# The complex feed-forward part of a transformer layer: three real products per tile instead of four

## What is computed

```python
xn = _layernorm(x)                                   # x: (32, 2048, 1024)
x = x + attn(xn) + ffn(xn)

# attn: 16 heads, causal, T = 2048
q1, q2, k1, k2 = (xn @ W.T for W in (W1_q, W2_q, W1_k, W2_k))     # 4 numbers per head each
L_q, L_k = exterior(q1, q2), exterior(k1, k2)        # 6 normalised numbers per head
attn = softmax(L_q @ (L_k @ J6.T).T * 6**-0.5, causal)
out = (attn @ (xn @ W_v.T + b_v)) @ W_out.T + b_out  # D = 1024

# ffn: a complex linear map, W_real and W_imag are 512 x 512, each unfolded from two small tensors
W_real, W_imag = unfold(G1_R, G2_R), unfold(G1_I, G2_I)
xr, xi = split(xn, 2, axis=-1)
out_real = xr @ W_real.T - xi @ W_imag.T + bias_real
out_imag = xr @ W_imag.T + xi @ W_real.T + bias_imag
ffn = concatenate([out_real, out_imag])
```

## Time and profile before

| | |
|---|---|
| runs of the kernel | 1768.63, 1771.18 (median) and 1957.53 us |
| the profiled execution, its own time | 1771.96 us |
| its span, first to last instruction, slowest core (core 1) | 1770.9 us |
| spans of the eight cores | 1757.7 to 1770.9 us |
| TensorE busy | 1582.8 us, 89% of the span |
| ScalarE busy | 1210.7 us, 68% |
| VectorE busy | 718.1 us, 41% |
| GpSimd busy | 172.5 us, 10% |

### The profile page before, as it was taken

How to read it: one execution, slowest core, us unless ns; L and a number is a source line. 1 busy time by engine, 2 the same in 40 slices (tenths; PEclk the granted TensorE clock), 3 DMA queues, 4 the chain that set the end, 5 groups by cost and what they waited for, 6 DMA issues and landing times.

```text
span 1770.9 us, 57248 instructions; the slowest of 8 cores (1757.7 to 1770.9 us)
## 1 busy us (share of the span) xinstructions
PE 1582.8 (89%) x24704; PEld 621.0 (35%) x24704; DVE 718.1 (41%) x1343; ACT 1210.7 (68%) x1408; POOL 172.5 (10%) x142
## 2 busy tenths in 40 slices
PE   3657999999988999999988999999997899999998
PEld 2323433333334443333334443333333443333332
DVE  5577534233245543333235553332226554321112
ACT  2434767878853668788774567878883466778786
POOL 1001110100011111000011110110001111012000
PEclk9978989999999999999999999999999999999999
DMA  9421522313235251321223442341223533122101
GB/s 203 97 74 38 117 65 64 88 55 68 73 79 133 73 145 38 97 61 37 75 83 103 122 109 71 75 103 37 56 61 91 145 79 79 38 62 85 38 25 49
DMA packets 159064, 141.20 MB, mean 80 GB/s; under 512 B 128224, under 2 KB 132448, under 8 KB 158816
## 3 DMA queue, kind: packets, MB, share of 16 engines
q1 hardware_dynamic: 154432, 132.75, 29.2%
q0 software_dynamic: 4384, 4.78, 1.8%
HBM read 78.32 MB, written 33.55 MB: 63 GB/s over the span
## 4 chain that ended last, share of the span: by engine, by line
PE 69%; DVE 11%; ACT 11%; issue 6%; DMA 2%; SPq 0%; DVEq 0%; ACTq 0%; POOL 0%; POOLq 0%
PE F L281 34%; PE S L596 14%; PE OA L635 8%; ACT ex L607 8%; PE DN L635 5%; PE OB L635 5%; DVE oT L656 3%; DVE xb L483 2%; DMA wqk<-wqkT 1%; DVE vt L430 1%; ACT rden L648 1%; ACT rden L646 1%; DVE qks L304 1%; DVE vt L519 1%; PE F L559 1%
## 5 line engine op out<-in xcount | busy, mean ns | idle before, releaser
L607 ACT ACTIVATE ex<-S 128x1024 bf16<-128x1024 f32 (+4 forms) x1055 | 1082.3, 1049 | 457.9 <-PE S L596 443.8
L596 PE MATMUL S<-fq,fk 6*128 6x512 bf16 (+3 forms) x2560 | 378.3, 357 | 42.7 <-ACT ex L607 40.4
L451 POOL TENSOR_TENSOR xb<-xb,outb 128x512 f32<-128x512 f32 x122 | 157.3, 1310 | 1506.9 <-DMA xb<-x 1506.9
L281 PE MATMUL F<-wv,xnT 128*32 128x512 bf16 x4096 | 265.1, 388 | 25.2 <-ACT vt L423 12.3
L281 PE MATMUL F<-wo,oT 128*32 128x512 bf16 x4024 | 268.0, 386 | 6.5 <-DVE oT L656 6.5
L635 PE MATMUL OA<-ex,vt 128*32 128x512 bf16 (+3 forms) x2560 | 238.9, 363 | 33.6 <-DVE ex L617 18.1
L596 PEld LDWEIGHTS S<-fq,fk 6*128 6x128 bf16 x2560 | 101.0, 91 | 453.3 <-issue 449.2
L635 PE MATMUL DN<-ex,ones 128*32 128x512 bf16 (+3 forms) x2560 | 235.1, 356 | 0.0
L483 DVE TENSOR_TENSOR xb<-F,xb 128x512 f32<-128x512 f32 x122 | 84.4, 691 | 370.3 <-PE F L281 356.1
L635 PE MATMUL OB<-ex,vt 128*32 128x512 bf16 (+3 forms) x2560 | 234.1, 355 | 0.0
L617 DVE TENSOR_TENSOR ex<-ex,tri 128x512 bf16<-128x512 bf16 x256 | 104.3, 419 | 232.2 <-ACT ex L607 231.7
(11 more groups left out here) (77 smaller groups left out, 844.2 us busy)
## 6 DMA issues: line engine op xcount, KB each, us to landing
xst<-x SPq DMA_DIRECT2D x62, 512.0 KB, 4.6
xb<-x SPq DMA_DIRECT2D x61, 512.0 KB, 4.3
y<-xb SPq DMA_DIRECT2D x60, 512.0 KB, 3.0
wv<-wvT POOLq DMA_DIRECT2D x4, 512.0 KB, 30.2
wo<-woP POOLq DMA_DIRECT2D x4, 512.0 KB, 39.4
ex<-x SPq DMA_DIRECT2D x3, 512.0 KB, 11.0
y<-xst SPq DMA_DIRECT2D x6, 256.0 KB, 2.2
oT<-x SPq DMA_DIRECT2D x2, 512.0 KB, 16.5
```

Source lines behind the costliest of these rows:

```text
L281: ins = TE.matmul(bank[32 * j:32 * j + 32, lo:hi], stationary[:, 32 * j:32 * j + 32], moving, start=start, stop=stop, tile_position=(0, 32 ...
L451: gS.inc(GE.tensor_tensor(r[:, h * 512:(h + 1) * 512], r[:, h * 512:(h + 1) * 512], outb[:, h * 512:(h + 1) * 512], OP.add))
L596: ins = TE.matmul(S[:, m * 512 + off:(m + 1) * 512], fk[32 * m:32 * m + 6, o:o + 128], fq[c % 2][32 * m:32 * m + 6, g * 512 + off:(g + 1) ...
L607: n = sS.inc(SE.activation(view(ex[i % 3], m0 * 512 + off, dims), view(S, m0 * 512 + off, dims), AF.Exp, scale=SCALE))
```

## The change

The complex product is made from three real ones. With `s = -(W_real + W_imag)` and `d = W_imag - W_real`, the common product `C = (xr + xi) @ W_real.T` goes to both halves: `out_real = C + xi @ s.T`, `out_imag = C + xr @ d.T`.

- `wi` and `wn` go, `ws` and `wd` come, and two small buffers `xs` for `xr + xi`.
- `xs_make` adds the two halves of a tile's `xnT` on VectorE (128 x 512, bf16).
- A new unit `common_unit`, one per tile, of 4 pieces, makes `C` in `F`; VectorE then adds the bank to both halves of the residual in one operation of 1024 columns, makes the next tile's `xs`, and only then `background` runs. The wait for the residual moves here from `out_add`.
- `out_products` has four feed-forward pieces instead of eight, so an `out_unit` has 12 instead of 16, an `early_unit` 8 or 10 instead of 12 or 14.
- `ffn_pieces` makes both parts of a block of the weights in five pieces and then `wr`, `ws`, `wd`.
- `choose` weighs the queues by pieces instead of units, takes a short unit (4 pieces or fewer) at the head of `outs` whenever it is asked, and no longer gives up where the head is not ready.

```diff
         def out_products(t, half, bank, groups, ffn):
...
             if ffn:
-                for kc in range(8):
-                    w = (wr, wi)[half] if kc < 4 else (wn, wr)[half]
-                    ins = by_columns(0, 512, xnT_of(t, kc), w[:, (kc % 4) * 512:(kc % 4) * 512 + 512],
-                                     kc == 0, False, bank)
+                for k in range(4):
+                    ins = by_columns(0, 512, xnT_of(t, k + 4 * (half == 0)),
+                                     (ws, wd)[half][:, k * 512:k * 512 + 512], k == 0, False, bank)
                     yield 1.0
...
+        def xs_make(t):
+            o = (t % CH) * 1024
+            x = xnT[(t // CH) % 4]
+            wait_for(VE, xt_in[t])
+            tS.wait(VE, xs_used.get(t - 2, 0))
+            xs_in[t] = vS.inc(VE.tensor_tensor(xs[t % 2][:], x[:, o:o + 512], x[:, o + 512:o + 1024], OP.add))
+
+        def common_unit(t):
+            vS.wait(TE, ffn_in[0])
+            vS.wait(TE, xs_in[t])
+            wait_for(TE, f_free[0])
+            for k in range(4):
+                ins = by_columns(0, 512, xs[t % 2][:, k * 128:k * 128 + 128], wr[:, k * 512:k * 512 + 512],
+                                 k == 0, k == 3)
+                if k == 3:
+                    xs_used[t] = tS.inc(ins)
+                yield 1.0
+            tS.wait(VE, tS.n)
+            gS.wait(VE, xb_in[t])
+            r = view(residual(t), 0, [[512, 2], [1, 512]])
+            n = vS.inc(VE.tensor_tensor(r, view(F, 0, [[0, 2], [1, 512]]), r, OP.add))
+            if t + 1 < NT:
+                xs_make(t + 1)
+            evicted((vS, n))
...
         def out_add(t, half, bank):
             tS.wait(VE, tS.n)
-            gS.wait(VE, xb_in[t])
...
+            def total(ri):
+                for half in (1024, 512):
+                    vS.wait(VE, vS.n)
+                    to = TERM + 1024 if half == 1024 else TERM + 512 * ri
+                    vS.inc(VE.tensor_tensor(fview(to, [[1, half]]), fview(TERM + 1024, [[1, half]]),
+                                            fview(TERM + 1024 + half, [[1, half]]), OP.add))
+                return True
...
+                vS.inc(VE.tensor_copy(w[0], re))
+                vS.inc(VE.scalar_tensor_tensor(w[1], re, -1.0, im, OP.mult, OP.subtract))
+                ffn_in[0] = vS.inc(VE.tensor_tensor(w[2], im, re, OP.subtract))
...
+            return [lambda: products(0), lambda: total(0), lambda: products(1), lambda: total(1), weights]
...
-                self.gen, self.left, self.ready = gen, cost, ready
+                self.gen, self.left, self.ready, self.short = gen, cost, ready, cost <= 4
...
-                    self.outs.extend(Unit(out_unit(prev * CH + t, h), 16.0)
-                                     for t in range(CH) for h in range(2))
+                    for t in range(prev * CH, prev * CH + CH):
+                        self.outs.append(Unit(common_unit(t), 4.0, lambda: not ffn))
+                        self.outs.extend(Unit(out_unit(t, h), 12.0, lambda: not ffn) for h in range(2))
...
-                        self.outs.extend(Unit(early_unit(t, h), 8.0 + 2 * n, lambda n=n: (c, n - 1) in o_in)
+                        self.outs.append(Unit(common_unit(t), 4.0))
+                        self.outs.extend(Unit(early_unit(t, h), 4.0 + 2 * n, lambda n=n: (c, n - 1) in o_in)
...
-                spare = len(self.outs) - self.ends
-                if self.outs and not self.outs[0].ready():
-                    return None
-                if self.outs and (end or not self.vs or 16 * spare > 8 * len(self.vs)):
+                ready = self.outs and self.outs[0].ready()
+                spare = sum(u.left for u in self.outs) - 14 * self.ends
+                if ready and (end or not self.vs or self.outs[0].short
+                              or spare > sum(u.left for u in self.vs)):
                     return self.outs.popleft()
-                for q in (self.vs, self.qk, self.outs):
+                for q in (self.vs, self.qk, self.outs if ready else None):
...
+            if c == 1:
+                xs_make(0)
```

More of the change, by code:

```diff
@@ L85, in build @@
         wr = sb("wr", 4 * 512, BF16)
-        wi = sb("wi", 4 * 512, BF16)
-        wn = sb("wn", 4 * 512, BF16)
+        ws = sb("ws", 4 * 512, BF16)
+        wd = sb("wd", 4 * 512, BF16)
+        xs = [sb(f"xs{i}", 512, BF16) for i in range(2)]
         xnT = [sb(f"xnT{i}", CH * 1024, BF16) for i in range(4)]
@@ L477, in out_products @@
                     yield 1.0
+        xs_in, xs_used = {}, {}
+        def xs_make(t):
[21 more added lines that the diff above has]
+            evicted((vS, n))
         def out_add(t, half, bank):
             tS.wait(VE, tS.n)
-            gS.wait(VE, xb_in[t])
             r = residual(t)[:, half * 512:half * 512 + 512]
@@ L509, in early_unit, with ffn_pieces, done, products @@
             evicted((vS, n))
-        def ffn_pieces(ri, j):
-            w = (wr, wi)[ri][:, j * 512:(j + 1) * 512]
-            def products():
+        def ffn_pieces(j):
+            def done():
+                return fview(TERM, [[1, 512]]), fview(TERM + 512, [[1, 512]])
+            def products(ri):
                 d_g2.wait(VE, d_g2.n)
-                vS.inc(VE.tensor_tensor(fview(TERM, [[512, 4], [16, 32], [1, 16]]),
+                vS.wait(VE, vS.n)
+                vS.inc(VE.tensor_tensor(fview(TERM + 1024, [[512, 4], [16, 32], [1, 16]]),
                                         fview(G1O + (ri * 4 + j) * 128, [[32, 4], [1, 32], [0, 16]]),
@@ L522, in products, with weights @@
                 return True
-            def pairs():
+            def total(ri):
+                for half in (1024, 512):
+                    vS.wait(VE, vS.n)
+                    to = TERM + 1024 if half == 1024 else TERM + 512 * ri
+                    vS.inc(VE.tensor_tensor(fview(to, [[1, half]]), fview(TERM + 1024, [[1, half]]),
+                                            fview(TERM + 1024 + half, [[1, half]]), OP.add))
+                return True
+            def weights():
+                re, im = done()
+                w = [t[:, j * 512:(j + 1) * 512] for t in (wr, ws, wd)]
                 vS.wait(VE, vS.n)
-                vS.inc(VE.tensor_tensor(fview(TERM + 2048, [[1, 1024]]), fview(TERM, [[1, 1024]]),
-                                        fview(TERM + 1024, [[1, 1024]]), OP.add))
-                return True
[L530 to L540, removed]
+                vS.inc(VE.tensor_copy(w[0], re))
+                vS.inc(VE.scalar_tensor_tensor(w[1], re, -1.0, im, OP.mult, OP.subtract))
+                ffn_in[0] = vS.inc(VE.tensor_tensor(w[2], im, re, OP.subtract))
+                return True
+            return [lambda: products(0), lambda: total(0), lambda: products(1), lambda: total(1), weights]
         def bias_unit():
@@ L727, in build @@
         lns.extend(ln_pipeline(range(CH, 2 * CH), True))
-        for ri in range(2):
-            for j in range(4):
-                ffn.extend(ffn_pieces(ri, j))
+        for j in range(4):
+            ffn.extend(ffn_pieces(j))
         background()
```

## The result

The changed kernel takes 1977 us against 1769: the ratio is 1.1177, with a 95% interval of 1.1131 to 1.1224. The forecast was 1910, the range 1840 to 1968. The direction and the place were right, the size was 67 us short and outside the range. Some executions of most of the kernels, the unchanged one too, are several per cent longer, with a lower granted clock on the cores of one die or of both; every ratio here compares executions without that, and e9 (two such executions) and e12 (one) therefore have times and no ratio.

A forecast was written before the change was run, and what follows sets the result against it. TensorE was taken to set the pace, with ScalarE near at w = 3. The terms: 1772 - 49 + 87 + 6 + 13 + 16 + 5 + 4 = 1854, plus 56 for the clock, 1910 us; range 1840 to 1968.

The forecast's parts named there:

- C before O in 31 group ends: Common unit ahead of the output unit at 31 group ends, TensorE idle 3.35 us; +87 outside w = 0, +13 there.
- The seven ends with C behind O8: At w = 2 and 3, common unit behind eight output-unit pieces at seven group ends: 2.6 us idle each, +16.
- all ends: All changed group ends, waits and clock falls together: 106 + 16 + 56 = 178 us.
- Pieces removed ... -49: Four pieces fewer per tile, 55.0 us of TensorE; a third of the 17 us at w = 3 lost: -49.
- eight ends with 4 pieces less: At w = 1, group ends that had 16 pieces now have 12 within the same wait: +6.
- the clock's 56: Clock falls behind the longer idle times at group ends: 33 falls at 1.7 us each, +56.
- 38 falls of 6.8: Upper end of the clock term: 38 falls of 6.8 us at 0.44 per us, 114 us.
- chunk 0's +4: The weights' unfolding in ffn_pieces: more VectorE work in chunk 0, between 0 and 7 us, taken as +4.
- -49 + 5 + 4 = -40: Pieces removed -49, further waits at w = 0 over three chunks +5, ffn_pieces in chunk 0 +4.

The follow-up runs named there:

- e9: Changed kernel without common units: each output unit makes the common product in its own bank, 16 pieces, old order; 1771.0 and 1773.4 us.
- e12: Kernel before with 12 pieces per output unit, half of the feed-forward products left out, nothing added; 1850 us in the profiled execution.
- e3: Kernel before with one wait added: at 31 group ends TensorE waits for normalize before going on with filler work; ratio 1.0814, 1912 us.
- e5: Changed kernel, but at group ends the output unit is taken and the common unit comes at a later step; ratio 1.0261, 1822 us.
- e2: Changed kernel with 14 idle matmuls between common and output unit at each of the 31 ends; ratio 1.0709, 1895 us.
- e7: Kernel before with 14 pieces per output unit, a quarter of the feed-forward products left out, nothing added; ratio 0.9993.
- e1: Changed kernel with a common unit that is first at a group's end issued, with its addition, ahead of normalize; ratio 1.0618, 1877 us.
- e8: Changed kernel with its order at the ends, but 16-piece output units and no common units at w = 3; ratio 1.0792, 1914 us.
- e4: Kernel before with ffn_pieces in the changed kernel's form; ratio 1.0007.
- e6: As e5, but output units at w = 3 make the common product in their own bank, 16 pieces, without common units; ratio 1.0221, 1812 us.
- e10: As e7, but output units at w = 3 and in the last chunk keep all 16 pieces; ratio 0.9891, 1748 us.

## Why the prediction was right and wrong

**Right: the order and what it does.** C before O in 31 group ends, its addition behind `normalize` (802.50 behind 801.90), idle for 3.31 against 3.35, the addition 1.21 long against 1.23. The seven ends with C behind O8 were taken too dear: TensorE waits 1.7 (w = 2) and 1.3 (w = 3) there, not 2.6, and no fall follows on any core. e3 puts the price of these gaps, clock included, at 144 us against 153; e5 puts all ends at 162 against 178.

**Right: the clock follows the gaps, at the price forecast.** e2 gives 0.33 per us at w = 1 (5.5 for 16.5), where the forecast took 0.38. At w = 3 the five of e2's 24 chunks that never fell take 149.9, against 165.9 with 41 us low in the changed kernel, whose delays are the same: 0.39; the line through all 24 of e2 has 0.41.

**Wrong: "Pieces removed ... -49".** This step failed. The term turned 256 x 0.215 us of TensorE into 49 us of the kernel, and asked only where ScalarE is near, not what the removal does to the clock. e7 measured -1 (between -10 and +7). Where the clock never fell, the pieces gave 2.8, 1.7, 2.4 and 2.5 of 3.4 us per chunk, and at w = 3 more than at w = 1; summed over the chunks that is 30 to 35 us, an estimate from the two tables. But the time at the lower level rose from 72 to 127 us per core, which at some 0.4 took 22 of it back, the largest part in the last chunk (7 us longer, 35 us low). And the cores spread: the slowest took 1767, the other seven 1743 to 1748. With twice as many pieces gone the sign turns (e12). So the pieces had been holding the clock up. I treated filler work as a load only. The sum has one more slip: eight ends with 4 pieces less are 6.9 us, not 6.

**Wrong by size: the clock's 56.** I counted 33 falls of 5.1 us, 168 us. Measured are 253 us more than before (325 less 72, mean of the cores). Each of the 31 gaps has a fall on each core, 6.1 long in the mean. 110 of the 253 lie in the three chunks at w = 3, which also have falls of over 15 us: 27 of them on the eight cores, 22 of which begin at key tile 4, three steps behind a group's end. In groups 0 and 2 of chunk 7 no kernel here has filler in the two steps between (key tiles 2 and 3), the kernel before neither; at key tile 4 the kernel before has 4 pieces, the changed one 1. These falls are in the changed kernel, e1, e2, e5 and e12 and hardly in the others. e8 prices w = 3 as a whole at 58 us. The forecast of 152 for such a chunk missed it by 14 (165.9), w = 1 (95 against 99.2) and w = 2 (122 against 125.9) by 4. The range ended at 38 falls of 6.8 and had no case in which a fall lasts 17 us, though the earlier trace rows has one of 13.7.

**Too high: chunk 0's +4.** e4: net about nothing (chunk 0 longer by 11, chunk 1 shorter by 8).

Put together from the measurements: the ends 162 (forecast 178), and 46 in what e5 has left, where the forecast had -49 + 5 + 4 = -40. By the mean of the cores what e5 has left is 51: w = 3 has 3 x 8.7 = 26, w = 0 3 x 2.9 = 9, w = 2 and 1 about 11, chunks 0 and 1 5. The whole is 208 us, where the forecast had 138. That the miss is only 70 is in part luck, errors of opposite sign: the ends were taken 16 too dear and the rest 86 too cheap, of which 48 are the pieces.

**What stays open.** Why e7 with as many pieces per chunk as the changed kernel has few long falls at w = 3, and e5 has them: the pieces are dealt to other steps, and which property of the dealing decides was not tried. Few pieces in single steps are not enough: in chunk 7 e7 has none at key tiles 2, 3 and 4 of groups 0 and 2, fewer than the changed kernel, and one long fall on eight cores. No run filled the thin steps at w = 3 with idle matmuls, as e2 did the gaps, so that thin filling causes the long falls is shown only by taking pieces away (e12) and putting them back (e6, e8), which also moves C. Falls also vary from core to core with the same instructions, as e2 and e12 show. No version of the product with common units beat the kernel before; e10 shows that at most about 1% was there to be had from as few pieces at w = 0, 1 and 2, and there the common units cost more than that (e6: 77.5, 84.9 and 116.1 against 72.2, 84.1 and 115.2).

## What to carry to other kernels

Before work is taken off the busiest engine, ask in each stage what ends last once it is gone, and try the saving alone, with nothing added: here 512 fewer pieces made the kernel slower, and 176 chosen by stage made it 1% faster. Look at the stretches in which the clock stayed up by themselves: they tell what the saving is worth, and the others what the clock took of it. A short unit in a single accumulator bank must not stand first where its emptying queues behind other work of the emptying engine; the cover there was not "some 12 pieces" but 12 pieces in one unit. And where the granted clock falls behind idle time, filler work at the seams is worth more than its own duration.

## What the runs showed of the chip that was not expected

- With 512 pieces gone, the mean clock of the cores went from 0.974 to 0.983 down to 0.898 to 0.955 and the time rose by 55 to 80 us. Leaving matmuls out is not free.
- In the changed kernel all 31 gaps of 2.9 to 5.8 us were followed by a fall, on each of the eight cores. Gaps of 1.0 to 1.8 us mostly were not: 5 of some 165 there, but about one in four of those of 1.4 to 1.8 us in e1. The price was 0.33 us per us at the lower level at w = 1 and 0.39 to 0.41 at w = 3. The Trainium skill ("TensorE: Matmul & The Clock Gate", Terms) puts it at a half; these rows are below that, probably since TensorE is not all of the path.
- The same page of the Trainium skill (Part 1) says that for modelling the ramp is under 1% of a typical span. It says so of the slow matmuls at the start, and the prediction took it for falls that come again after every gap. For those it does not hold here: holding the clock up in the gaps (e2) took 83 us, over 4%, off the changed kernel.
- 14 matmuls at each of the 31 ends, into a half of `S` that would be overwritten anyway, shortened the kernel by those 83 us, though nothing uses their results.
